# A mixture-of-experts block: first quad prepared ahead of the last choice, tables of experts in other places

## The chip, the cores and the metric

The kernel runs on one core of a Trainium2 chip. The metric is the device time of one execution in microseconds (us). The core's engines are TensorE (PE in the profile, its weight loads PEld), VectorE (DVE), ScalarE (ACT), GpSimd (POOL) and SyncE (SP); each runs its own program in order, and they wait for each other on semaphores. SPq and POOLq are the queues on which SyncE and GpSimd issue transfers.

## The reference, cut to what matters

```python
def attention(x):                      # x: (8, 64, 256), per image, after a normalisation over channels
    kq = w_kq @ x + b_kq; v = w_v @ x + b_v
    ctx = softmax(kq.T @ kq) @ v.T
    return w_o @ ctx + b_o
x = x + attention(ln_c(x))
t = tokens(x)                          # 2048 tokens of 64 channels
flat = ln_t(t)
probs = softmax(flat @ router_w.T)     # 8 experts
top 2 experts per token, their probabilities divided by their sum -> gates
y_e = w2[e] @ (silu(w1[e] @ flat) * (w3[e] @ flat))     # hidden 682, per chosen expert
t = t + sum over the two chosen e of gate_e * y_e
```

## The kernel before

**Attention stage.** The 8 images are handled in 4 pairs. Per pair `p`: statistics, transposes, the product `kq`, `similarity`, for each image `b` a `row_max(b)` on VectorE, `exponentials(b)` on ScalarE, `transpose_probs(b)` and `attend(b)` on TensorE, then on VectorE `residual(b)` (which gives the tokens and the router's logits), `t_statistics(p)`, `tops(b)`, `choose(p)`; TensorE's `rank(p)` counts each token's place within its expert, `positions(p)` makes row numbers, `normalise_t(p)` the normalised tokens. GpSimd computes the deviations (`t_deviation(p)`) and scatters the tokens with `scatter_row(p, at)`, 8 indirect transfers a pair, to a buffer `xs` in HBM that is sorted by expert.

**Expert stage.** The rows of `xs` are worked on in subtiles of 128 rows, each of one expert; there are up to 39, in 10 quads of four, and a round is the work on one quad. Round `i`: `pair_up(i)` on VectorE copies the loaded rows `x_in` twice side by side into `x_pairs`, `turn_x(i)` transposes them on TensorE, `columns(i)` copies them to `x_cols` on ScalarE. Then six steps `s` of `up(6i+s)` on TensorE, `silu` on ScalarE and `multiply` on VectorE, then `down(i)` on TensorE (L1061), ScalarE's `y_copy(i)` (L513), TensorE's `turn_y(i)`, VectorE's `results(i)` and GpSimd's four `scatter_result`. `up(g)` waits for the product `g-3`, so TensorE runs at most three steps ahead of VectorE.

**Tables.** Which expert a subtile has (`owners`), and where its rows begin (`rows`), is known as counts become known. There are three phases: after pair 1 eight subtiles (quads 0, 1), after pair 2 eight more (quads 2, 3), after pair 3 the rest. A phase's tables are VectorE chains of small operations: `subtiles_of_experts` (L659 to L670), `owners_of_slots` (L675, L678), `jumps_between_owners`, `rows_of_slots` (to L696 or L701), and `used_up` (L706, L707) ahead of a later phase. The first phase's are made at the start of pair 2, the second's at the end of pair 3 ahead of `pair_up(1)` and of `normalise_t(3)`, the third's in rounds 0 and 1.

**SyncE** waits for a phase's tables (`table_ready`) and reads row numbers and owners from the table into registers, four of each for a quad (`rows_of`, `owners_of`); it issues the four loads of rows (L293, 32.5 KB each) once the scatters of that phase have landed (`landed(p)`), and then the quad's four weight loads (L277, 565 KB each). There are buffers for the weights of three quads and the rows of four. All these transfers are on SyncE's queue.

**TensorE around the last choice.** After `attend(7)`: `keep_busy(4)` (products without a use, L959), `rank(3)`, `keep_busy(3)`, then `turn_x(0)`, `keep_busy(1)` and the rounds. `turn_x(i+1)` follows step 1 in round 0 and step 0 in later rounds, on ScalarE `columns(i+1)` likewise.

## Time and profile before

| | us |
|---|---|
| median of 3 runs | 174.97 |
| lowest, highest | 174.4, 175.56 |
| the profiled execution | 175.2 |
| its span | 173.1 |
| busy: PE, PEld | 144.0, 120.4 |
| busy: DVE, ACT, POOL | 97.8, 71.5, 85.7 |

The span is the time from the first to the last instruction that the profile holds; the device time has about 2 us more around it. An engine's busy share is an average over stages with different limits, so a change in a stage is read from that stage: from the instructions' order in time, and from the idle time ahead of them with the engine and line that ended it (`[0.83 <-DMA x_in<-xs]` is 0.83 us of idleness, ended by a transfer into x_in). PEclk is the granted clock of TensorE, 1.00 for 2.4 GHz and 0.50 for 1.2 GHz. Products in fp32 are pipelined, so that several overlap.

### The profile page before, as it was taken

To read this page: it belongs to the slowest core of one execution; us is meant where nothing else is said; L and a number is where in the kernel's file an instruction comes from. 1 tells how busy PE (TensorE), PEld (TensorE's weight loads), DVE (VectorE), ACT (ScalarE), POOL (GpSimd) and SP (SyncE) were. 2 spreads that over 40 slices of the span, in tenths; PEclk is the share of its full clock that TensorE was granted. 3 is DMA by queue.
4 is the path that set the end of the run, shared out by engine and by line. 5 is a ranking of instruction groups with operands and counts; after the bars stand their busy time and mean duration, and the time that the engine had idled before them with its cause. 6 is when DMAs were issued, how large, how long until landed. Compare 5 with 4: busy or idle time off the path is not lost.

```text
span 173.1 us, 4872 instructions
## 1 busy us (share of the span) xinstructions
PE 144.0 (83%) x1682; PEld 120.4 (70%) x1682; DVE 97.8 (57%) x364; ACT 71.5 (41%) x141; POOL 85.7 (50%) x114
## 2 busy tenths in 40 slices
PE   0669949578788699899699999999999999984782
PEld 0446737367277279797598989899999999874262
DVE  0645695785762888769554646455555736443050
ACT  2148666241144037253363636363545454542011
POOL 2685427887771477777071625344343526356000
PEclk9999997955555579999999999999999999999698
DMA  4999400100882492279896979596969981010434
GB/s 117 326 287 296 107 0 15 31 19 27 238 340 55 106 399 110 58 193 397 249 370 189 378 226 376 168 398 159 386 174 366 278 326 38 5 31 15 113 137 121
DMA packets 19892, 32.99 MB, mean 191 GB/s; under 512 B 7691, under 2 KB 13100, under 8 KB 19868
## 3 DMA queue, kind: packets, MB, share of 16 engines
q1 hardware_dynamic: 16732, 29.55, 52.6%
q0 software_dynamic: 2272, 2.35, 4.2%
q10 hardware_dynamic: 864, 0.79, 1.5%
q8 instruction: 13, 0.21, 0.5%
q14 instruction: 11, 0.09, 0.2%
HBM read 25.55 MB, written 7.13 MB: 189 GB/s over the span
## 4 chain that ended last, share of the span: by engine, by line
issue 30%; POOL 26%; PE 22%; DVE 9%; DMA 5%; ACT 5%; POOLq 1%; SPq 0%; DVEq 0%; ACTq 0%
POOL ys L366 20%; PE psum L927 7%; POOL xs L357 5%; PE psum L916 4%; PE psum L896 3%; ACT xn L422 2%; DMA y_in<-ys 2%; PE psum L1105 2%; PE psum L887 2%; DMA proj<-projections 1%; PE psum L882 1%; DMA ys<-y_out,y_row 1%; DVE parts L620 1%; ACT probsT L456 1%; DVE rows L591 1%
## 5 line engine op out<-in xcount | busy, mean ns | idle before, releaser
L366 POOL DMA_INDIRECT ys<-y_out,y_row x39 | 37.4, 958 | 45.3 <-DVE y_out L839 36.2
L1033 PE MATMUL psum<-x_cols,weights 64*128 64x128 f32 x390 | 49.5, 279 | 1.6 <-DMA weights<-experts 1.2
L1035 PE MATMUL psum<-x_cols,weights 64*128 64x128 f32 x390 | 49.7, 279 | 0.0
L1033 PEld LDWEIGHTS psum<-x_cols,weights 64*128 64x128 f32 x390 | 45.6, 188 | 5.7 <-issue 3.8
L827 DVE TENSOR_TENSOR hid<-psum,act_sb 128x512 f32<-128x512 f32 (+1 forms) x50 | 33.8, 677 | 23.4 <-ACT act_sb L500 23.1
L1035 PEld LDWEIGHTS psum<-x_cols,weights 64*128 64x128 f32 x390 | 45.7, 188 | 0.0
L500 ACT ACTIVATE act_sb<-psum 128x512 f32<-128x512 f32 (+1 forms) x50 | 29.3, 587 | 25.2 <-PE psum L1033 24.7
L357 POOL DMA_INDIRECT xs<-xrows,pos x32 | 31.6, 988 | 11.6 <-issue 8.6
L1061 PE MATMUL psum<-hid,weights 128*64 128x128 f32 x468 | 28.8, 276 | 0.2 <-DVE hid L827 0.2
L1061 PEld LDWEIGHTS psum<-hid,weights 128*64 128x64 f32 x468 | 25.9, 137 | 2.0 <-DVE hid L827 0.4
L927 PEld LDWEIGHTS psum<-u_sb,probsT 128*128 128x128 f32 x64 | 11.3, 266 | 5.2 <-ACT probsT L456 2.8
L927 PE MATMUL psum<-u_sb,probsT 128*128 128x73 f32 x64 | 12.3, 358 | 2.9 <-ACT probsT L456 1.6
L959 PE MATMUL psum<-ones,before 128*128 128x512 bf16 x24 | 10.3, 577 | 3.5 <-issue 3.5
L513 ACT COPY y_cols<-psum 128x256 f32<-128x256 f32 (+1 forms) x10 | 3.6, 362 | 21.2 <-PE psum L1061 21.2
L779 DVE COPY x_pairs<-x_in 128x512 f32<-128x512 f32 (+1 forms) x10 | 4.4, 438 | 11.0 <-DMA x_in<-xs 11.0
L448 ACT ACTIVATE probs<-psum,neg_max 128x256 f32<-128x256 f32 x16 | 6.7, 474 | 9.3 <-DVE neg_max L580 9.3
L492 ACT COPY x_cols<-psum 128x512 f32<-128x512 f32 (+1 forms) x10 | 5.7, 575 | 8.4 <-PE psum L1015 8.4
L456 ACT COPY probsT<-psum 128x512 f32<-128x512 f32 x8 | 4.7, 586 | 9.5 <-PE psum L916 9.5
L959 PEld LDWEIGHTS psum<-ones,before 128*128 128x128 bf16 x24 | 2.9, 133 | 7.9 <-issue 7.7
L916 PE MATMUL psum<-ident,probs 128*128 128x128 f32 x32 | 8.0, 401 | 0.3 <-ACT probs L448 0.3
L1015 PE MATMUL psum<-ident,x_pairs 128*128 128x128 f32 x39 | 6.9, 301 | 1.6 <-DVE x_pairs L779 1.6
L422 ACT ACTIVATE xn<-x_sb,shift_x,rstd 128x64 f32<-128x64 f32 x16 | 5.7, 428 | 5.9 <-DVE std L565 5.9
(147 smaller groups left out, 178.4 us busy)
## 6 DMA issues: line engine op xcount, KB each, us to landing
weights<-experts SPq DMA_DIRECT2D x39, 565.0 KB, 4.8
xs<-zeros SPq DMA_DIRECT2D x4, 1040.0 KB, 11.9
x_in<-xs SPq DMA_DIRECT2D x39, 32.5 KB
ys<-y_out,y_row POOLq DMA_INDIRECT x39
xs<-xrows,pos POOLq DMA_INDIRECT x32, 2.3
y_in<-ys ACTq DMA_DIRECT2D x2, 256.0 KB, 4.6
y_in<-ys SPq DMA_DIRECT2D x2, 256.0 KB, 4.4
x_sb<-x_tok SPq DMA_DIRECT2D x1, 384.0 KB, 3.8
```

Of the source, the lines that this page charges most:

```text
L357: nc.gpsimd.indirect_dma_start(xs, bass.IndirectOffsetOnAxis(ap=pos[:, p, at:at + 1], axis=0), xrows[:, TPP * p + at // K_TOP, at % K_TOP, ...
L366: nc.gpsimd.indirect_dma_start(ys, bass.IndirectOffsetOnAxis(ap=y_row[:, j:j + 1], axis=0), y_out[:, i % RING, h, :], None).then_inc(y_sca ...
L422: ins = nc.scalar.activation(xn[:, p, i, m, :], x_sb[:, t, :], ACT.Identity, bias=shift_x[:, t:t + 1], scale=rstd[:, t:t + 1])
L500: nc.scalar.activation(live(i, act_sb[:, g % 3, :]), live(i, H1_BANK[g % 2]), ACT.Silu).then_inc(silu_done, 1)
L827: nc.vector.tensor_tensor(live(i, hid[:, i % 2, s, :]), live(i, H3_BANK[g % 3]), live(i, act_sb[:, g % 3, :]), ALU.mult).then_inc(hid_done, 1)
L916: ins = nc.tensor.transpose(PT_BANK[:, N * j + P * i:N * j + P * (i + 1)], probs[:, b % 2, i, P * j:P * (j + 1)], ident[:])
L927: ins = nc.tensor.matmul(O_BANK[b % 2][:, (TX + 1) * i:(TX + 1) * (i + 1)], probsT[:, b % 2, j, P * i:P * (i + 1)], u_sb[:, 2 * b + j, E:] ...
L959: nc.tensor.matmul(bank[4], before[:], ones[:].unsqueeze(1).to_broadcast([P, BLK // P, P]), start=True, stop=True)
L1015: ins = nc.tensor.transpose(X_BANK[:, P * h:P * (h + 1)], x_pairs[:, i % 2, h, :, :], ident[:])
L1033: first_ = nc.tensor.matmul(H1_BANK[g % 2][:, src], weights[0:C, slot, P * s:P * (s + 1)], x_cols[0:C, i % 2, src], start=True, stop=True)
L1035: second_ = nc.tensor.matmul(H3_BANK[g % 3][:, src], weights[C:P, slot, P * s:P * (s + 1)], x_cols[C:P, i % 2, src], start=True, stop=True)
L1061: ins = nc.tensor.matmul(Y_BANK[C * (h % 2):C * (h % 2 + 1), P * (h // 2):P * (h // 2 + 1)], weights[:, slot, HP + C * s:HP + C * (s + 1)] ...
```

## The change

- The first phase's tables move from the start of pair 2 into pair 1, between the first two and the last two tiles of `normalise_t(1)`, and so ahead of `row_max(5)`.
- A new semaphore `owners_ready` rises when a phase's owners are known. SyncE loads the weights of quad 0 on it, one owner and one load at a time, and the weights of quad 2 on it, ahead of the row numbers and the row loads of quad 2.
- `pair_up(0)` moves ahead of `t_statistics(3)`; on TensorE `turn_x(0)` and `keep_busy(2)` come ahead of `rank(3)`; `keep_busy(3)` and `keep_busy(1)` go.
- The second phase's tables are made in pieces behind the products of steps 0 to 3 of round 0; `normalise_t(3)` moves behind step 5 of round 0. The third phase's `jumps` and `rows` move one step on in round 1.
- `pair_up(2)` moves from the end of round 0 behind step 2 of round 1; `turn_x(2)` and `columns(2)` move from step 0 to step 4 of round 1.
- GpSimd makes the deviation of pair 3 after all scatters of pair 2, where it was made after two of them.

```diff
@@ -54,6 +54,7 @@
 YROWS = PARK + NS * SUB
 WQUADS = 3
 WSLOTS = WQUADS * QUAD
+TURNED_AT = {0: 1, 1: 4}
 XRING = 4
 RING = 4
 ZW = E * CAP * RW // (QUARTERS * P * 8)
@@ -188,7 +189,7 @@
         dispatched = [sem(f"dispatched{p}") for p in range(PHASES)]
         variance_t_ready, rstd_t_ready = sem("variance_t_ready"), sem("rstd_t_ready")
         shifted, exponents, gates_ready = sem("shifted"), sem("exponents"), sem("gates_ready")
-        keep_ready, table_ready = sem("keep_ready"), sem("table_ready")
+        keep_ready, owners_ready, table_ready = sem("keep_ready"), sem("owners_ready"), sem("table_ready")
 
         w_loaded = [sem(f"w_loaded{i}") for i in range(WSLOTS)]
         x_in_loaded = [sem(f"x_in_loaded{i}") for i in range(XRING)]
@@ -295,21 +296,29 @@
             def landed(p):
                 sp.wait_ge(dispatched[p], 16 * TPP * K_TOP * (KNOWN[p] - (KNOWN[p - 1] if p else 0)))
 
+            sp.wait_ge(owners_ready, 1)
+            for h in members(0):
+                owner = sp.value_load(table[0:1, 0, h:h + 1], min_val=0, max_val=E - 1)
+                sp.dma_start(weights[:, h, :], experts[bass.ds(owner, 1)].rearrange("o p c -> p (o c)")).then_inc(w_loaded[h], 16)
             sp.wait_ge(table_ready, 1)
-            load_weights(0, owners_of(0))
             early_rows, second_owners = [rows_of(0), rows_of(1)], owners_of(1)
             landed(0)
             load_rows(0, early_rows[0])
             load_rows(1, early_rows[1])
             load_weights(1, second_owners)
             for p in range(1, PHASES):
+                sp.wait_ge(owners_ready, p + 1)
+                opening = quads_of(p)[0]
+                if opening < WQUADS:
+                    load_weights(opening, owners_of(opening))
                 sp.wait_ge(table_ready, p + 1)
                 for i in quads_of(p):
                     at = rows_of(i)
-                    if i == quads_of(p)[0]:
+                    if i == opening:
                         landed(p)
                     load_rows(i, at)
-                    load_weights(i, owners_of(i))
+                    if i >= WQUADS:
+                        load_weights(i, owners_of(i))
 
             all_scattered(sp)
             for q in range(0, QUARTERS, 2):
@@ -404,11 +413,11 @@
             t_deviation(0)
             for p in range(PAIRS):
                 for at in range(TPP * K_TOP):
-                    if p == 0 and at == TPP * K_TOP - 2 or p == 2 and at == K_TOP:
-                        t_deviation(p + 1)
+                    if p == 0 and at == TPP * K_TOP - 2:
+                        t_deviation(1)
                     scatter_row(p, at)
-                if p == 1:
-                    t_deviation(2)
+                if 1 <= p < PAIRS - 1:
+                    t_deviation(p + 1)
             for j in range(NS):
                 scatter_result(j)
 
@@ -521,7 +530,7 @@
                     y_copy(i - 1)
                 for s in range(STEPS):
                     silu(STEPS * i + s)
-                    if s == (1 if i == 0 else 0) and i + 1 < NQ:
+                    if s == TURNED_AT.get(i, 0) and i + 1 < NQ:
                         columns(i + 1)
             y_copy(NQ - 1)
             nc.scalar.preload_act_table(ACT.Exp)
@@ -623,9 +632,9 @@
                     ins = nc.vector.bn_aggr(moments_t[:, t, :], parts[:, 1, t, :])
                 ins.then_inc(moments_t_ready, 1)
 
-            def normalise_t(p):
+            def normalise_t(p, part=range(TPP)):
                 dve.wait_ge(rstd_t_ready, p + 1)
-                for t in range(TPP * p, TPP * (p + 1)):
+                for t in (TPP * p + i for i in part):
                     ins = nc.vector.tensor_scalar(xrows[:, t, :, 0:C], rows[:, t:t + 1, E:TX].to_broadcast([P, K_TOP, C]),
                                                   moments_t[:, t, 0:1], rstd_t[:, t:t + 1], ALU.subtract, ALU.mult)
                     ins.then_inc(tn_ready, 1)
@@ -675,8 +684,7 @@
                 chain(nc.vector.tensor_tensor(passed[:, own, :], slot_at[:, own].unsqueeze(2).to_broadcast([P, n, E - 1]),
                                               ends[:, 1:E].unsqueeze(1).to_broadcast([P, n, E - 1]), ALU.is_ge))
                 with nc.allow_low_precision(reason="numbers of experts: whole and below 2^3"):
-                    nc.vector.tensor_reduce(table[:, 0, own], passed[:, own, :], AX.X, ALU.add).then_inc(dve_step, 1)
-                steps[0] += 1
+                    nc.vector.tensor_reduce(table[:, 0, own], passed[:, own, :], AX.X, ALU.add).then_inc(owners_ready, 1)
 
             def jumps_between_owners(p):
                 if p == 0:
@@ -787,33 +795,31 @@
                     nc.vector.copy_predicated(y_row[:, own], keep[:, own], ids).then_inc(y_row_ready, 1)
 
             for p in range(PAIRS):
-                if p == KNOWN[0]:
-                    subtiles_of_experts(0)
-                    owners_of_slots(0)
-                    jumps_between_owners(0)
-                    rows_of_slots(0)
                 if p >= 1:
                     x_logits(p)
                 residual(2 * p)
                 tops(2 * p)
                 residual(2 * p + 1)
+                if p == PAIRS - 1:
+                    pair_up(0)
                 t_statistics(p)
                 if p + 1 < PAIRS:
                     row_max(2 * p + 2)
                 tops(2 * p + 1)
                 choose(p)
                 carry_on(p)
-                if p == PAIRS - 1:
-                    pair_up(0)
                 positions(p)
                 if p == PAIRS - 1:
-                    used_up(0)
-                    subtiles_of_experts(1)
-                    owners_of_slots(1)
-                    jumps_between_owners(1)
-                    rows_of_slots(1)
                     pair_up(1)
-                normalise_t(p)
+                if p == KNOWN[0] - 1:
+                    normalise_t(p, range(2))
+                    subtiles_of_experts(0)
+                    owners_of_slots(0)
+                    jumps_between_owners(0)
+                    rows_of_slots(0)
+                    normalise_t(p, range(2, TPP))
+                elif p < PAIRS - 1:
+                    normalise_t(p)
                 if p + 1 < PAIRS:
                     row_max(2 * p + 3)
 
@@ -840,14 +846,26 @@
                                       ).then_inc(y_out_ready, 1)
 
             def tables_between(i, s):
-                if (i, s) == (0, 5):
+                if (i, s) == (0, 0):
+                    used_up(0)
+                    subtiles_of_experts(1)
+                elif (i, s) == (0, 1):
+                    owners_of_slots(1)
+                elif (i, s) == (0, 2):
+                    jumps_between_owners(1)
+                elif (i, s) == (0, 3):
+                    rows_of_slots(1)
+                elif (i, s) == (0, 5):
+                    normalise_t(PAIRS - 1)
                     used_up(1)
                     subtiles_of_experts(2)
                 elif (i, s) == (1, 1):
                     owners_of_slots(2)
                 elif (i, s) == (1, 2):
+                    pair_up(2)
+                elif (i, s) == (1, 3):
                     jumps_between_owners(2)
-                elif (i, s) == (1, 3):
+                elif (i, s) == (1, 4):
                     rows_of_slots(2)
                 elif (i, s) == (1, 5):
                     occupancy(2)
@@ -860,7 +878,7 @@
                     if s == 0 and i >= 1:
                         results(i - 1)
                     tables_between(i, s)
-                if i + 2 < NQ:
+                if 1 <= i < NQ - 2:
                     pair_up(i + 2)
             results(NQ - 1)
 
@@ -1002,8 +1020,6 @@
                 if p + 1 < PAIRS:
                     similarity(p + 1)
             keep_busy(4)
-            rank(PAIRS - 1)
-            keep_busy(3)
 
             def turn_x(i):
                 pe.wait_ge(x_paired, i + 1)
@@ -1078,11 +1094,12 @@
             pe.wait_ge(probs_ready, B)
             pe.wait_ge(t_ready, B)
             turn_x(0)
-            keep_busy(1)
+            keep_busy(2)
+            rank(PAIRS - 1)
             for i in range(NQ):
                 for s in range(STEPS):
                     up(STEPS * i + s)
-                    if s == (1 if i == 0 else 0) and i + 1 < NQ:
+                    if s == TURNED_AT.get(i, 0) and i + 1 < NQ:
                         turn_x(i + 1)
                     if s == 0 and i >= 1:
                         turn_y(i - 1)
```

## Rows read from the trace of the kernel before

**Rows 1.** Timeline, ScalarE: the copy that closes a round (columns: start, duration, instruction, idle)

```profile
93.00 0.37 ACT L513 COPY y_cols<-psum 128x256 f32<-128x256 f32 x1 [2.05 <-PE psum L1061]
...
101.97 0.37 ACT L513 COPY y_cols<-psum 128x256 f32<-128x256 f32 x1 [2.05 <-PE psum L1061]
...
120.48 0.37 ACT L513 COPY y_cols<-psum 128x256 f32<-128x256 f32 x1 [2.05 <-PE psum L1061]
```

**Rows 2.** Windows: busy us (instructions) of each engine, PEclk, DMA share, GB/s

```profile
22.60:24.60 2.00, 0.00 (x0) 0.03 (x1) 1.86 (x14) 2.00 (x6) 1.27 (x2) 1.00 0.00 0
25.30:28.20 2.90, 2.76 (x12) 2.35 (x12) 2.04 (x8) 1.41 (x4) 1.58 (x2) 0.50 0.02 7
...
35.40:62.20 26.80, 21.77 (x109) 15.12 (x105) 18.40 (x105) 7.26 (x14) 16.56 (x18) 0.50 0.48 151
...
62.50:154.50 92.00, 88.83 (x1378) 82.01 (x1379) 55.01 (x124) 43.67 (x78) 45.93 (x48) 1.00 0.70 239
```

**Rows 3.** The page's part 5: pairing of the rows (busy, mean ns; idle before it)

```profile
L779 DVE COPY x_pairs<-x_in 128x512 f32<-128x512 f32 (+1 forms) x10 | 4.4, 438 | 11.0 <-DMA x_in<-xs 11.0
```

**Rows 4.** Timeline, SyncE's queue: loads of the rows and weights

```profile
68.64 2.58 SPq L293 DMA_DIRECT2D x_in<-xs  x4
73.62 2.16 SPq L277 DMA_DIRECT2D weights<-experts  x4
78.21 1.90 SPq L293 DMA_DIRECT2D x_in<-xs  x4
```

**Rows 5.** Timeline, VectorE: rounds 1 and 2

```profile
72.88 0.43 DVE L779 COPY x_pairs<-x_in 128x512 f32<-128x512 f32 x1 [0.83 <-DMA x_in<-xs]
...
77.78 0.16 DVE L685 TENSOR_TENSOR begin<-used,base 128x8 f32<-128x8 f32 x1
...
80.65 0.68 DVE L830 TENSOR_TENSOR hid<-psum,act_sb 42x512 f32<-42x512 f32 x1
...
84.53 0.43 DVE L779 COPY x_pairs<-x_in 128x512 f32<-128x512 f32 x1 [1.68 <-DMA x_in<-xs]
```

**Rows 6.** Timeline, TensorE: around rounds 0 to 2

```profile
55.93 1.91 PE L959 MATMUL psum<-ones,before 128*128 128x512 bf16 x4
...
62.48 0.46 PE L1033 MATMUL psum<-x_cols,weights 64*128 64x128 f32 x1 [0.25 <-ACT x_cols L492]
...
68.57 2.84 PE L1061 MATMUL psum<-hid,weights 128*64 128x128 f32 x48
...
83.24 0.34 PE L1033 MATMUL psum<-x_cols,weights 64*128 64x128 f32 x1 [1.21 <-DMA weights<-experts]
```

**Rows 7.** Timeline, VectorE: the end of pair 1 and the first tables

```profile
36.17 1.11 DVE L629 TENSOR_SCALAR xrows<-rows,moments_t,rstd_t 128x128 f32<-128x128 f32 x4
37.19 0.68 DVE L580 TENSOR_REDUCE neg_max<-psum 128x2 f32<-128x512 f32 x1
37.79 0.28 DVE L659 SCALAR_TENSOR_TENSOR over<-taken_by,steps_sub 128x128 f32<-128x128 f32 x1
...
40.01 0.17 DVE L696 TENSOR_TENSOR table<-row_at,slot_at 128x8 int32<-128x8 f32 x1
```

**Rows 8.** Timeline, ScalarE: exponentials of image 5, first silu

```profile
38.16 0.85 ACT L448 ACTIVATE probs<-psum,neg_max 128x256 f32<-128x256 f32 x2
...
63.75 0.60 ACT L500 ACTIVATE act_sb<-psum 128x512 f32<-128x512 f32 x1 [1.33 <-PE psum L1033]
```

**Rows 9.** Chain that ended last: transposes of image 5

```profile
40.31 0.87 PE psum L916 x4
```

**Rows 10.** Timeline, VectorE: last choice, tables of phase 1, first products

```profile
58.90 0.19 DVE L614 TENSOR_TENSOR taken<-chosen 128x32 bf16<-128x32 f32 x1
...
60.31 0.16 DVE L706 TENSOR_SCALAR given<-ends 128x8 f32<-128x8 f32 x1
...
62.33 0.21 DVE L678 TENSOR_REDUCE table<-passed 128x8 int32<-128x56 f32 x1
...
65.32 1.27 DVE L827 TENSOR_TENSOR hid<-psum,act_sb 128x512 f32<-128x512 f32 x2
```

## The prediction

> **What bounds the kernel now.** Read the copies that close a round first: one round is the work on one quad of subtiles, and ScalarE copies its output at the end [rows 1]. From 93.00 to 101.97 a round takes 8.97 us, and TensorE has no gap in it: the windows view shows 88.83 us busy of 92 from 62.5 to 154.5, at full clock [rows 2]. So ten rounds, most of them bound by TensorE. The next two rounds, 101.97 to 120.48, take 18.51 where 2 x 8.97 = 17.94 would do. They lose 0.57 us. The page's costliest groups say to what: VectorE stood 11.0 us in all for x_in, the rows of the coming quads [rows 3].
>
> So read SyncE's queue [rows 4]. Per quad it reads four row numbers, issues four row loads (x_in), reads four owners, issues four weight loads. From the end of the weights at 73.62 + 2.16 = 75.78 to 78.21 lie the four register loads: 2.43 us, 0.61 each. A whole turn (row loads 1.90, weights 2.16, twice 2.43 and the wake-ups) is 9 to 9.5 us, as long as a round or longer: a second, hidden bound. A quad's rows come late as well, for they are issued behind the previous quad's weights: those of quad 3 are issued from 78.21 and VectorE gets them at 84.53, 6.3 us later [rows 5]. The rows of quad 2, issued from 68.64 with no weights ahead of them, were there at 72.88, 4.2 us later [rows 4, 5].
>
> Third, the places that lose time around the first rounds. TensorE starts round 0 at 62.48, ends it at 68.57 + 2.84 = 71.4, and starts round 2 at 83.24, held 1.21 us by weights [rows 6]. GpSimd's scatters of pair 2 stop in the middle, behind a deviation whose moments are late.
>
> **The change, part by part.** (1) *First tables ahead of row_max(5).* The tables take 37.79 to 40.18, 2.39 us [rows 7]. They now lie between two halves of normalise_t(1) (1.11 us for four, so 0.57 a half), and row_max(5) is queued behind all: 36.17 + 0.57 + 2.39 + 0.5 gives 39.6, plus 0.66 gives 40.25, where it ended at 37.87. Who waits: the exponentials of image 5 ran at 38.16 for 0.85 [rows 8] and now run at 40.28 to 41.12; the transposes of them started at 40.31, set by TensorE [rows 9], and now start at 41.16. The cover was 1.3 us, the delay is 2.4: all that follows in the attention stage comes **0.85 us later**, since this is the chain of waits. SyncE gets the first owners 1 us earlier and issues the first weights and rows earlier; nobody waited for either (rounds 0 and 1 show no wait for them), so this gains 0.
>
> (2) *pair_up(0) ahead of t_statistics(3)*: 0.43 and a copy of ids, 0.46 us together, on VectorE [rows 5], earlier, so the last choice comes 0.85 + 0.46 = 1.31 later: taken at 58.90 + 0.19 + 1.31 = 60.40 [rows 10].
>
> (3) *TensorE.* keep_busy(4) ended at 57.84 [rows 6], now 58.7. turn_x(0) follows directly (about 0.9), ScalarE's copy ends at about 60.2, keep_busy(2) fills until 60.4, rank(3) starts at 60.55 and takes 0.35. Round 0 starts at **60.9 instead of 62.48**, 1.6 us sooner. That is the visible gain.
>
> (4) *Tables of phase 1 between the products of round 0.* VectorE: positions 0.5 from 60.95, pair_up(1) 0.5, then silu(0) (63.75 + 0.60 was 1.87 after the round's start [rows 8]) ends at 62.8. multiply(0) 0.62, as two took 1.27 [rows 10]; used_up and subtiles; multiply(1) 0.62; owners. The two table parts were 60.31 to 62.54, 2.23 us [rows 10]. So owners_ready rises at 62.8 + 0.62 + 2.23 + 0.62 = **66.25**. The products are then late by the tables' time; round 0 ends on VectorE's last product at about 70.9 against 71.4. Of 1.6 us only 0.5 is left here. Then normalise_t(3) (1.1) and used_up(1) with subtiles(2) (2.0) delay the first product of round 1 to 73.3.
>
> (5) *SyncE's order.* From 66.25: four owners 2.65 (with the wake-up), four weights 2.15, four row numbers 2.43, so the rows of quad 2 are issued from **73.5; before, from 68.64** [rows 4]. The weights of quad 2 leave at 68.9 instead of 73.62, and the 1.21 us wait at 83.24 goes. But the rows are now behind 2.26 MB of weights. With the 6.3 us of quad 3's rows they are there at **79.8**. The bounds: 4.2 us, as in the empty queue (77.7), and 7.0 (80.5).
> The Trainium skill, "DMA: Bandwidth & Descriptors", section "Queues, rings and completion order", says that descriptors of one ring are consumed in ring order, which speaks against this reordering; by it the small rows wait for all the weights, as the trace's 6.3 us shows, and the sum is the one made here.
>
> (6) *turn_x(2) after step 4 of round 1, pair_up(2) after step 2.* VectorE reaches pair_up(2) at 73.3 + three products, results and owners(2) = 76.2 and stands until 79.8. Queued behind it are the products of steps 3, 4 and 5 and the tables of phase 2. Before, jumps, three products and rows took 77.78 to 80.65 + 0.68 = 81.33 [rows 5], 3.55 us; now 79.8 + 0.41 + 3.55 = 83.8, and the last sixth of down(1) (2.84 / 6) gives 84.3. TensorE has done up of steps 0 to 4 by 75.9 and stands until 80.25: **a gap of 4.3 us that was not there.**
>
> (7) *GpSimd.* The stop in pair 2 is closed, but pair 3's scatters now wait for normalise_t(3) at 71.3 and end at 81.4, 4 us later than before; results of quad 0 follow until 86.5, ahead of quad 1's. SyncE needs the scatters at 87. Worth 0 while these covers hold; without them each scatter is 1.26 us.
>
> **What the gap costs.** A gap of 2.0 us (22.6 to 24.6) was followed by a clock of 0.50, that is 1.2 GHz, although TensorE was 95% busy after it; work was back at 24.6 and 28.2 still shows 0.50, so the low clock held for 3.6 us of work or a little more [rows 2]. So a gap of 4.3 us most likely brings 1.2 GHz. Work left in round 1 at 80.25: transposes 0.5, tail 0.6, down 2.84 = 3.95 us at full clock. Each us at half clock does half a us. If the clock returns 3 to 4 us after work resumes (I take 3.6), the round ends at 80.25 + 3.95 + 1.8 = **86.0**. Hot it would be 84.3, by VectorE.
> The Trainium skill, "TensorE: Matmul & The Clock Gate", section "HAM oscillation — how this bites in real kernels", has waits for DMA bring the half clock as well; the trace's much shorter gap agrees. By that rule the sum stays the one with the half clock.
>
> **The sum.** Round 2 starts at 86.0; quad 3's rows are issued at 77.85 and are long there. Round 2 takes 8.97 and closes at 95.0; before at 93.00: +2.0. SyncE's issues from quad 3 on stay where they were (77.85 against 78.21), so with TensorE later its two late row loads no longer show: -0.57. The end moves by **+1.4 us**. The profiled execution took 175.2 us with a span of 173.1, so 176.6; against the median 174.97 it is 0.2 slow. Forecast 174.97 + 1.4 = **176.4 us**.
>
> **Rivals.** *A, the clock stays up*: 84.3, then quad 3's pairs at 85.7 hold the turn 0.5 us, round 2 closes at 93.75, +0.75 - 0.57 = +0.2: 175.2. For it: full clock since 62.5. Against: the 2.0 us gap. *B, the rows of quad 2 are not held by the weights* (77.7 or sooner): no long gap, round 2 starts at 82 or earlier. But then TensorE runs into SyncE's turn in rounds 3 to 5, and SyncE is only 0.35 us ahead of before: 174.6. Against: 6.3 us at 84.53. *C, the other side, slower by over 1%: the half clock lasts.* Place: down(1), after the gap. Price: 0.5 us per us. It decides from 4.3 us of half clock on, where the sum passes +1.75; until 86.9 it gives +2.95, and if round 0 also starts at half clock (60.9 lies in the stretch that ran at 0.50, [rows 2]) VectorE's first product, and all behind it, is 0.75 later: +3.7, 178.7. Typical 177.6. For it: from 35.4 to 62.2 the clock stayed at 0.50 with TensorE busy 21.77 of 26.8 us. *D, faster by over 1%*: the 1.6 us of the start and the losses of rounds 1 and 2 (83.24 - 62.48 - 2 x 8.97 = 2.8) are all kept: up to 170.6. For it: the weights wait goes. Against: SyncE's turn would have to shrink too, and it is four loads and four issues twice over as before.
>
> **How the numbers follow.** Forecast 0.36, A 0.10, B 0.06, C 0.38, D 0.10. One per cent, 1.75 us, is about what a measurement tells here. Forecast, A and B are within it: 0.52; C slower: 0.38; D faster: 0.10. The range runs from B, 174.6, less nothing, to C with nearly all its terms, 178.4; it leaves out D and the rest of C, under 0.2. The likeliest case's own range is 175.9 to 176.7.
>
> **What would show it.** Right: the transposes of image 5 at 41.2; up of round 0 at 60.9; weights of quad 2 issued at 69 and its rows at 73.5; x_pairs waiting over 3 us for x_in before 80 in round 1; a TensorE gap of 4 us there and a clock below 1.00 behind it; round 2 starting between 85 and 87; no x_in wait on TensorE in rounds 4 and 5. Wrong: rows of quad 2 there by 78; owners_ready before 65; SyncE's turn under 9 us; round 6 starting before 120.

## The result and the profile after

| | us |
|---|---|
| median before, 20 runs | 176.65 (173.26 to 180.43) |
| median after, 20 runs | 177.84 (174.97 to 180.70) |
| ratio after / before | 1.0099, 95% interval 1.0051 to 1.0148 |
| profiled execution after, its span | 178.76, 177.0 |

The change makes the kernel about 1% slower; 0.8% was forecast (1.4 us of 174.97). Over 20 runs both kernels scatter by 3 to 4%, so the ratio, not the two medians, is the result. The ratio and its interval, here and below, compare only the executions of each kernel that lie within 1.5% of its fastest; the medians of all 20 stand at 1.0067.

The profiled execution of after has 3.9 us more span than that of before; it is read for where time goes, not for how much in the median. Only 2.36 us of the 3.9 are there at the end of round 5. The other 1.5 lie behind the last round, where the 32 transposes of the result took 5.34 us instead of 3.84, at a granted clock of 0.50 until 171.7. That isn't the change: a second profile of after has them at 3.84 again.

The profiled executions differ by up to 2.3 us (31.0 to 33.3) at the start of residual(3), ahead of all that was changed. So marks are also counted from one of their own execution, **residual(7)**: the start of VectorE's work on image 7, the last, at 56.24 before and at 56.81 after.

```profile
56.24 0.17 DVE L586 RECIPROCAL inv_sum<-psum 128x2 f32<-128x2 f32 x1 [2.11 <-PE psum L927]
```

```profile
56.81 0.17 DVE L595 RECIPROCAL inv_sum<-psum 128x2 f32<-128x2 f32 x1 [2.11 <-PE psum L945]
```

ScalarE's copies that close a round in the kernel after, which answer to [rows 1]:

```profile
70.25 0.37 ACT L522 COPY y_cols<-psum 128x256 f32<-128x256 f32 x1 [2.42 <-PE psum L1077]
...
86.96 0.37 ACT L522 COPY y_cols<-psum 128x256 f32<-128x256 f32 x1 [4.19 <-PE psum L1077]
...
95.93 0.37 ACT L522 COPY y_cols<-psum 128x256 f32<-128x256 f32 x1 [2.05 <-PE psum L1077]
...
104.90 0.37 ACT L522 COPY y_cols<-psum 128x256 f32<-128x256 f32 x1 [2.05 <-PE psum L1077]
...
122.84 0.37 ACT L522 COPY y_cols<-psum 128x256 f32<-128x256 f32 x1 [2.05 <-PE psum L1077]
```

Before closed its first two rounds here:

```profile
71.46 0.37 ACT L513 COPY y_cols<-psum 128x256 f32<-128x256 f32 x1 [2.05 <-PE psum L1061]
...
82.08 0.37 ACT L513 COPY y_cols<-psum 128x256 f32<-128x256 f32 x1 [2.67 <-PE psum L1061]
```

Round 0 closes at 70.25. Round 1 closes at 86.96, 16.7 us later, where before needed 10.6. From then on every round takes 8.97 us: round 2 closes at 95.93, 2.9 us behind before's 93.00, and round 5 at 122.84, 2.36 us behind 120.48. The 0.57 us that before lost in rounds 4 and 5 is what came back.

SyncE's queue after, against [rows 4] (the first row is the weights of quads 1 and 2, the second the rows of quads 2 and 3, merged by the view):

```profile
54.02 16.37 SPq L278 DMA_DIRECT2D weights<-experts  x8
72.81 6.29 SPq L294 DMA_DIRECT2D x_in<-xs  x8
81.50 2.16 SPq L278 DMA_DIRECT2D weights<-experts  x4
```

The rows of quad 2 are issued at 72.81, 4.2 us later than before. VectorE after, around the last choice, in round 0 and in round 1, against [rows 10] and [rows 5]:

```profile
57.52 0.42 DVE L787 COPY x_pairs<-x_in 128x512 f32<-128x512 f32 x1
...
59.76 0.19 DVE L623 TENSOR_TENSOR taken<-chosen 128x32 bf16<-128x32 f32 x1
...
62.25 0.69 DVE L833 TENSOR_TENSOR hid<-psum,act_sb 128x512 f32<-128x512 f32 x1 [0.76 <-ACT act_sb L509]
...
65.46 0.21 DVE L687 TENSOR_REDUCE table<-passed 128x8 int32<-128x56 f32 x1
...
74.62 0.68 DVE L833 TENSOR_TENSOR hid<-psum,act_sb 128x512 f32<-128x512 f32 x1
79.29 0.44 DVE L787 COPY x_pairs<-x_in 128x512 f32<-128x512 f32 x1 [4.00 <-DMA x_in<-xs]
...
82.80 0.68 DVE L836 TENSOR_TENSOR hid<-psum,act_sb 42x512 f32<-42x512 f32 x1
```

pair_up(0) is at 57.52, ahead of the choice (taken at 59.76). The owners are known at 65.46 + 0.21 = 65.67. In round 1 VectorE ends a product at 75.3 and stands 4.00 us for x_in, in the middle of the round; the round's last product comes at 82.80. TensorE after, against [rows 6]:

```profile
60.46 0.34 PE L1049 MATMUL psum<-x_cols,weights 64*128 64x128 f32 x1
...
79.79 1.11 PE L1031 MATMUL psum<-ident,x_pairs 128*128 128x128 f32 x4 [4.29 <-DVE x_pairs L787]
```

Round 0 begins at 60.46, and in round 1 TensorE stands for the pairs until 79.79, 4.29 us by the row. Windows after (us, busy of PE, PEld, DVE, ACT, POOL with instructions, granted clock, DMA share, GB/s), against [rows 2]:

```profile
76.00:79.70 3.70, 0.00 (x0) 0.00 (x0) 0.41 (x2) 0.12 (x1) 2.79 (x4) 0.97 0.68 196
80.00:86.00 6.00, 6.00 (x50) 5.41 (x51) 5.18 (x18) 1.18 (x2) 4.08 (x5) 0.50 0.63 200
...
86.50:154.00 67.50, 67.50 (x1067) 62.69 (x1064) 36.09 (x68) 33.96 (x62) 28.38 (x30) 1.00 0.71 242
```

TensorE is idle to 79.7; then come 6 us of work without a break at 0.50, 1.2 GHz, and 1.00, 2.4 GHz, from 86.5 on. Cut finer, the windows show the clock fall at 79.5, while TensorE still stood, and come back at 86.3. The last sixth of down(1) could have come behind VectorE's last product at 83.5; it ended at 86.9.

Ends of rounds behind residual(7), in us, for the kernels that the text turns on. "Filled" and "GpSimd's order" are experiments below.

| | profiles | round 1 | round 2 | round 5 |
|---|---|---|---|---|
| before | 1 | 25.8 | 36.8 | 64.2 |
| after | 2 | 30.2, 29.7 | 39.1, 38.7 | 66.0, 65.6 |
| after, gap filled | 2 | 27.4, 27.9 | 36.6, 37.1 | 63.5, 64.0 |
| after, GpSimd's order back | 2 | 27.8, 29.2 | 36.8, 38.2 | 63.7, 65.1 |
| before, GpSimd's order alone | 1 | 25.2 | 34.3 | 61.4 |

### The profile page after: what moved, and what is told of

The parts are those of the page before. It is cut to its first block, busy times and chain, and to the rows that moved or that the text cites. A ratio compares the mean times of both kernels' runs of the same rounds, so it can differ in the third digit from the quotient of the medians.

```text
span 177.0 us, 4868 instructions
## 1 busy us (share of the span) xinstructions
PE 146.8 (83%) x1680; PEld 124.1 (70%) x1680; DVE 97.2 (55%) x364; ACT 71.4 (40%) x141; POOL 86.2 (49%) x114
## 4 chain that ended last, share of the span: by engine, by line
issue 30%; POOL 24%; PE 21%; DVE 12%; ACT 5%; DMA 4%; POOLq 1%; SPq 0%; DVEq 0%; ACTq 0%
POOL ys L375 20%; PE psum L945 6%; POOL xs L366 4%; PE psum L934 4%; PE psum L1122 3%; ACT xn L431 2%; DMA y_in<-ys 2%; PE psum L914 2%; DVE hid L833 2%; PE psum L905 2%; PE psum L900 1%; DMA ys<-y_out,y_row 1%; DMA proj<-projections 1%; ACT probsT L465 1%; DVE neg_max L589 1%
## 5 line engine op out<-in xcount | busy, mean ns | idle before, releaser
L833 DVE TENSOR_TENSOR hid<-psum,act_sb 128x512 f32<-128x512 f32 (+1 forms) x50 | 33.9, 677 | 33.3 <-ACT act_sb L509 32.9
L1077 PE MATMUL psum<-hid,weights 128*64 128x128 f32 x468 | 30.8, 288 | 0.0
L1077 PEld LDWEIGHTS psum<-hid,weights 128*64 128x64 f32 x468 | 28.1, 145 | 1.9 <-issue 0.3
L977 PE MATMUL psum<-ones,before 128*128 128x512 bf16 x22 | 8.1, 514 | 3.5 <-issue 3.5
L1031 PEld LDWEIGHTS psum<-ident,x_pairs 128*128 128x128 f32 x39 | 4.7, 156 | 6.1 <-DVE x_pairs L787 4.5
```

The lines of the kernel that those rows point to most:

```text
L833: nc.vector.tensor_tensor(live(i, hid[:, i % 2, s, :]), live(i, H3_BANK[g % 3]), live(i, act_sb[:, g % 3, :]), ALU.mult).then_inc(hid_done, 1)
L977: nc.tensor.matmul(bank[4], before[:], ones[:].unsqueeze(1).to_broadcast([P, BLK // P, P]), start=True, stop=True)
L1031: ins = nc.tensor.transpose(X_BANK[:, P * h:P * (h + 1)], x_pairs[:, i % 2, h, :, :], ident[:])
L1077: ins = nc.tensor.matmul(Y_BANK[C * (h % 2):C * (h % 2 + 1), P * (h // 2):P * (h // 2 + 1)], weights[:, slot, HP + C * s:HP + C * (s + 1)] ...
```

## The experiments

All ratios are to the kernel before, measured beside it. A difference between two of them is read with both intervals in mind.

**The gap filled.** In the kernel after, TensorE runs 16 products without a use in the gap:

```diff
+                    if (i, s) == (1, 4):
+                        pe.wait_ge(x_cols_ready, 2)
+                        for _ in range(16):
+                            nc.tensor.matmul(X_BANK, before[:], ones[:].unsqueeze(1).to_broadcast([P, BLK // P, P]),
+                                             start=True, stop=True)
                     if s == TURNED_AT.get(i, 0) and i + 1 < NQ:
                         turn_x(i + 1)
```

> The changed kernel with 16 products without a use put on TensorE between step 4 of round 1 and turn_x(2), that is into the 4 us gap. Theory (the gap costs by its half clock): the granted clock stays 1.00 through rounds 1 and 2, round 1 closes at about 84.5 instead of 86.96, set by VectorE's last product, round 2 at about 93.9; time against the kernel before 1.001 to 1.003. Rival (the late rows alone cost the time, the clock does not matter): round 1 closes at 86.5 or later as in the changed kernel, ratio 1.01.

Measured: 1.0030 (0.9967 to 1.0094). A window and the close of round 1 in it:

```profile
80.00:86.00 6.00, 5.44 (x77) 4.61 (x78) 5.49 (x20) 1.84 (x4) 4.35 (x5) 1.00 0.58 171
...
84.63 0.37 ACT L522 COPY y_cols<-psum 128x256 f32<-128x256 f32 x1 [2.22 <-PE psum L1077]
```

The clock stays at 1.00 over the whole round. VectorE still stands 4.06 us for x_in and makes the pairs at 79.91, later than after's 79.29, yet the round closes 2.3 us sooner: 4.7 us behind the pairs instead of 7.7. So between these two profiles 3 us of round 1 are the clock's. The late rows by themselves leave round 1 closing 27.4 us behind residual(7), where before closed it after 25.8. But that is made up again: round 2 closes at 36.6 (before 36.8) and round 5 at 63.5 (before 64.2). The gap without its half clock costs nothing by round 5, and what is left of the loss is made ahead of residual(7), by the first tables (1.06 us, below).

A second time, beside the kernel after itself:

> The changed kernel with the TensorE gap of round 1 filled, a second time, beside the changed kernel. Theory (the half clock behind the gap is most of the loss): 0.5 to 1.2 per cent below the changed kernel, clock 1.00 through rounds 1 and 2. Rival: the same as the changed kernel.

> The changed kernel itself, beside the next two on one chip. Theory: a TensorE gap of about 4 us in round 1 and 3.4 to 6.8 us of half clock behind it, the length by chance from execution to execution; ratio 1.003 to 1.012.

Measured: filled 1.0035 (0.9980 to 1.0091), after 1.0050 (1.0000 to 1.0099). The order is the expected one both times, but the second difference, 0.15%, is less than expected and far inside the intervals; over both sessions it is 0.4% (1.0033 against 1.0075). The second profiles say the same as the first: filled, the clock stays at 1.00 and round 1 closes 5.0 us behind its pairs; in after TensorE stands 3.75 us, the clock is 0.50 from 80.2 to 87.0, and the round closes 7.4 us behind its pairs. That the half clock happens and what it costs in one execution is shown by the profiles; what share of the median it is stays uncertain.

**First tables back behind row_max(5)**, all else as after:

```diff
             for p in range(PAIRS):
+                if p == KNOWN[0]:
+                    subtiles_of_experts(0)
+                    owners_of_slots(0)
+                    jumps_between_owners(0)
+                    rows_of_slots(0)
                 if p >= 1:
                     x_logits(p)
...
-                if p == KNOWN[0] - 1:
-                    normalise_t(p, range(2))
-                    subtiles_of_experts(0)
-                    owners_of_slots(0)
-                    jumps_between_owners(0)
-                    rows_of_slots(0)
-                    normalise_t(p, range(2, TPP))
-                elif p < PAIRS - 1:
+                if p < PAIRS - 1:
                     normalise_t(p)
```

> The changed kernel with the first phase's tables back behind row_max(5). Theory (the tables delay row_max(5) and by it the attention stage by 0.85 us): the transposes of image 5 start with no wait for the exponentials, all later marks 0.8 to 1 us earlier, ratio 1.003 to 1.005. Rival (the sooner first tables pay by earlier weights and rows of quads 0 and 1): ratio above 1.01, a wait on weights or rows in round 0 or 1.

Measured: 0.9988 (0.9930 to 1.0045). Starts of residual(4) and residual(5) on VectorE, of before, of after and then of this kernel:

```profile
40.42 0.16 DVE L586 RECIPROCAL inv_sum<-psum 128x2 f32<-128x2 f32 x1
...
43.93 0.17 DVE L586 RECIPROCAL inv_sum<-psum 128x2 f32<-128x2 f32 x1 [2.02 <-PE psum L927]
```

```profile
39.93 0.16 DVE L595 RECIPROCAL inv_sum<-psum 128x2 f32<-128x2 f32 x1
...
44.50 0.17 DVE L595 RECIPROCAL inv_sum<-psum 128x2 f32<-128x2 f32 x1 [3.09 <-PE psum L945]
```

```profile
41.27 0.16 DVE L595 RECIPROCAL inv_sum<-psum 128x2 f32<-128x2 f32 x1
...
44.71 0.17 DVE L595 RECIPROCAL inv_sum<-psum 128x2 f32<-128x2 f32 x1 [1.97 <-PE psum L943]
```

From 39.93 to 44.50 are 4.57 us; from 41.27 to 44.71, 3.44. Before had 3.51. So the tables ahead of row_max(5) cost 1.1 us in the chain, and nothing was gained by having them sooner: no wait for the weights or rows of quads 0 and 1 shows up here. The ratio fell by 1.1%, more than the 0.6% that 1.1 us is, and below the 1.003 to 1.005 expected; the intervals leave room for that. Its profile also had a shorter half clock in round 1, 80.5 to 84.0, against 79.5 to 86.3 in after's, which this edit doesn't explain; so the 1.1% need not be all the tables'.

**Second phase's tables back in one piece** ahead of pair_up(1), all else as after:

> The changed kernel with the second phase's tables back in one piece at the end of pair 3, ahead of pair_up(1); all else as changed. Theory (late tables make the rows of quad 2 late): owners_ready about 2 us earlier (near 63.5), rows of quad 2 issued near 71 instead of 72.8 and paired near 77.2 instead of 79.3, the TensorE gap in round 1 about 2 us instead of 4, end 2 us or more earlier than the changed kernel, ratio 0.995 to 1.000. Rival (pieces cost nothing, since the weights of quad 2 set the end of round 1): ratio 1.01 as the changed kernel.

Measured: 1.0241 (1.0148 to 1.0335), a miss. The owners were known sooner (6.4 us behind residual(7), against 8.9 in after), and the rows of quad 2 came without a wait (pairs at 80.64, 21.6 us behind residual(7), against 22.5 in after). But pair_up(1) stood behind the tables until 66.78, and TensorE, which now starts round 0 early, stood 2.6 us for it and worked at half clock behind it: round 0 closed at 75.67, 16.7 us behind residual(7) instead of 13.4. normalise_t(3), which stays behind round 0, went with it. GpSimd's first scatter of pair 3, and SyncE's weight loads of quad 3 and row loads of quad 4, which wait for these scatters (3.2 us, by the view of SyncE's waits from 84 to 95; none in after):

```profile
74.89 1.27 POOL L366 DMA_INDIRECT xs<-xrows,pos  x1 [11.25 <-DVE xrows L638]
...
80.89 2.04 SPq L278 DMA_DIRECT2D weights<-experts  x4
90.08 2.97 SPq L294 DMA_DIRECT2D x_in<-xs  x4
```

The scatters begin 15.9 us behind residual(7) instead of 13.2, the rows of quad 4 are issued at 90.08, their weights behind them, and TensorE stands 2.49 us for the weights of quad 4: round 3 closes at 103.51, round 4 at 115.06, 11.55 us later. So the pieces in round 0 do buy something, once TensorE starts early: they let pair_up(1) and the products through. The kernel tests both together and does not price the pieces alone.

**SyncE's order for quad 2 back**, rows first, tables left as after:

```diff
-                if opening < WQUADS:
-                    load_weights(opening, owners_of(opening))
                 sp.wait_ge(table_ready, p + 1)
...
-                    if i >= WQUADS:
-                        load_weights(i, owners_of(i))
+                    load_weights(i, owners_of(i))
```

> The changed kernel with SyncE's order for quad 2 as before: its rows first, on table_ready, then its weights; the tables stay in pieces and late. Theory (what is late is SyncE's whole turn, since owners and rows of phase 1 are known later; the order only chooses who waits): rows of quad 2 issued near 70.5 and paired near 75.5 without a stall of VectorE, but the weights of quad 2 issued near 75 and landed near 83.5 to 84.5, so TensorE waits over 2.5 us for them at the start of round 2; ratio 1.005 to 1.015. Rival (the order of the two loads is what costs): no wait above 1 us in rounds 1 and 2, ratio below 1.0.

Measured: 1.0176 (1.0098 to 1.0255), a little above the range expected. SyncE's issues, and TensorE's start of round 2:

```profile
71.19 1.89 SPq L294 DMA_DIRECT2D x_in<-xs  x4
75.48 2.08 SPq L278 DMA_DIRECT2D weights<-experts  x4
```

```profile
86.16 0.55 PE L1046 MATMUL psum<-x_cols,weights 64*128 64x128 f32 x1 [5.74 <-DMA weights<-experts]
```

The rows are issued 14.0 us behind residual(7) instead of 16.0 and are paired at 75.64 without a wait; round 1 closes at 80.47. Then TensorE stands 5.74 us for the weights, and the clock is 0.50 from 83.1 to 89.9. So the swap in SyncE's order is not the fault: with tables this late the new order is no worse, and by the ratios (1.0176 against 1.0099 and 1.0050) the better of two. What is late is SyncE's whole turn.

**GpSimd's order alone**, in the kernel before:

```diff
-                    if p == 0 and at == TPP * K_TOP - 2 or p == 2 and at == K_TOP:
-                        t_deviation(p + 1)
+                    if p == 0 and at == TPP * K_TOP - 2:
+                        t_deviation(1)
...
-                if p == 1:
-                    t_deviation(2)
+                if 1 <= p < PAIRS - 1:
+                    t_deviation(p + 1)
```

> The kernel before with only GpSimd's order changed: the deviation of pair 3 after all scatters of pair 2. Theory (SyncE's turn is a second bound, and it started late because the scatters of pair 2 landed at 68.6): rows of quad 2 issued near 66.4 instead of 68.6, all of SyncE's issues 2.2 us earlier, no weights wait at the start of round 2, rounds from 3 on closing 2 to 2.5 us earlier, ratio 0.985 to 0.99. Rival (TensorE alone is the bound): only the start of round 2 changes, by at most 1.2 us, ratio 0.994 to 1.000.

Measured: **0.9846 (0.9764 to 0.9927), faster than both kernels**; median 172.75. SyncE's queue and the rounds' copies:

```profile
65.87 1.89 SPq L293 DMA_DIRECT2D x_in<-xs  x4
70.17 1.92 SPq L277 DMA_DIRECT2D weights<-experts  x4
74.53 1.93 SPq L293 DMA_DIRECT2D x_in<-xs  x4
78.86 2.34 SPq L277 DMA_DIRECT2D weights<-experts  x4
84.03 1.90 SPq L293 DMA_DIRECT2D x_in<-xs  x4
```

```profile
80.94 0.37 ACT L513 COPY y_cols<-psum 128x256 f32<-128x256 f32 x1 [2.67 <-PE psum L1061]
...
90.05 0.37 ACT L513 COPY y_cols<-psum 128x256 f32<-128x256 f32 x1 [2.05 <-PE psum L1061]
...
99.02 0.37 ACT L513 COPY y_cols<-psum 128x256 f32<-128x256 f32 x1 [2.05 <-PE psum L1061]
```

Before, the first three of these issues were at 68.64, 73.62, 78.21, and SyncE's row loads waited for scatters, 2.3 us of it ahead of 68.64:

```profile
SPq L293 <- DMA xs<-xrows,pos: 2.8, 2, 2.3
```

(us in total, times, the longest.) With GpSimd's order changed no such wait is left ahead of the rows of quad 2, the weights of quad 2 are there in time, and round 2 closes at 90.05 instead of 93.00, 34.3 us behind residual(7) instead of 36.8. A change of a few lines on GpSimd, which was busy for half of the span, is worth 2.7 us, because SyncE's turn hangs on it. The two experiments below that hold this order as well gave 0.986 and 0.983.

**GpSimd's order back in the kernel after**, twice:

> The changed kernel with GpSimd's order as before (deviation of pair 3 after two scatters of pair 2). Theory (in the changed kernel the scatters of pair 2 have landed long before SyncE gets to the rows of quad 2 at 72.8, so the new order brings nothing there): pair 2's scatters end near 68.5, the rows are still issued near 72.8, rounds close as in the changed kernel, ratio 1.005 to 1.015. Rival (GpSimd's order is worth its 1.5 per cent in the changed kernel too): ratio 1.02 or more.

> The changed kernel with GpSimd's order as before, a second time, beside the changed kernel. Theory (the order brings nothing there; the first ratio of 0.998 came from a shorter half clock in those executions): the same ratio as the changed kernel within 0.006. Rival (the new order costs the changed kernel something): again 0.8 to 1.2 per cent below it.

Measured: 0.9978 (0.9926 to 1.0031), then 1.0038 (0.9983 to 1.0093) beside after's 1.0050. In the profiles the rows of quad 2 are issued at 73.42 and 74.61, 16.0 and 16.6 us behind residual(7), as in after (16.0). So in the kernel after the order brings nothing: pair 2's scatters are not what SyncE waits for ahead of these rows. The rival, a ratio of 1.02 or more, is refuted. The first ratio lay below the range expected and 1.2% under after's; in that profile the clock was 0.50 from 79.9 to 83.3 only, against 79.5 to 86.3 in after's. Side by side the difference was gone, and the second profile had 79.1 to 85.9.

**The start alone** (pair_up(0), turn_x(0), keep_busy(2) and rank(3) moved as in the change), in the kernel before, and with GpSimd's order:

> The kernel before with the start alone (pair_up(0) ahead of t_statistics(3), turn_x(0) and keep_busy(2) ahead of rank(3)). Theory: as with GpSimd's order beside it, round 0 starts 1.5 to 2 us sooner and closes no sooner, SyncE's issues stay where they were or 0.3 us later, ratio 1.000 to 1.008. Rival (the start is gained): ratio 0.992 or lower.

> The kernel before with two parts of the change: GpSimd's order, and the start (pair_up(0) ahead of t_statistics(3), turn_x(0) and keep_busy(2) ahead of rank(3)); all tables as before. Theory (the second bound is SyncE and VectorE's tables, so an earlier start of round 0 brings nothing): round 0 starts 1.5 to 2 us sooner, TensorE then stands over 2 us for the pairs of quad 1, which wait behind the tables, tables and SyncE are 0.46 us later, and the end is 0.3 to 1.5 us later than with GpSimd's order alone, ratio 0.987 to 0.995. Rival (the start is gained): ratio 0.978 or lower.

Measured: 0.9996 (0.9959 to 1.0033) and 0.9861 (0.9790 to 0.9933), so the start is worth nothing on either while the tables stay in one piece. TensorE in the second:

```profile
64.61 0.66 PE L1013 MATMUL psum<-ident,x_pairs 128*128 128x128 f32 x4 [2.53 <-DVE x_pairs L779]
```

It starts round 0 early and then stands 2.53 us for the pairs of quad 1, which wait behind the tables on VectorE. Round 0 closes 15.35 us behind residual(7), where before closed it after 15.22.

**The attention stage filled**: GpSimd's order, and `keep_busy(12)` instead of `keep_busy(3)` ahead of the ranks of pairs 1 and 2:

> The kernel before with GpSimd's order, and with 12 products without a use instead of 3 ahead of the ranks of pairs 1 and 2, in the two places of the attention stage where TensorE stands 2.3 and 1.2 us for VectorE's choice. Theory (a gap of 2 us and more brings the half clock, as in round 1 of the changed kernel, and the half clock from 35 to 62 costs more than the gap itself): the clock stays 1.00 from 28 to 60, the attention stage ends 2 us or more earlier, ratio 0.965 to 0.98. Rival (the attention stage is set by the chain over VectorE and ScalarE, or its products do not hold the clock anyway): the clock falls near 38 to 45 all the same, then the added products at half clock delay the ranks by about 2 us, ratio 0.99 to 1.005.

Measured: 0.9831 (0.9749 to 0.9914), no different from GpSimd's order alone. Windows and TensorE in it:

```profile
33.00:41.00 8.00, 6.15 (x47) 3.73 (x43) 7.30 (x40) 3.28 (x7) 6.06 (x7) 1.00 0.07 21
42.00:44.50 2.50, 2.50 (x13) 1.12 (x13) 2.19 (x18) 0.00 (x0) 1.89 (x3) 0.50 0.09 27
45.00:51.50 6.50, 4.59 (x35) 2.97 (x33) 3.48 (x19) 1.85 (x4) 4.99 (x6) 1.00 0.93 342
52.00:64.00 12.00, 8.99 (x44) 5.71 (x46) 7.85 (x51) 3.09 (x5) 8.02 (x9) 0.50 0.50 139
```

```profile
43.48 3.52 PE L959 MATMUL psum<-ones,before 128*128 128x512 bf16 x12
...
52.68 1.11 PE L916 MATMUL psum<-ident,probs 128*128 128x128 f32 x4 [2.28 <-ACT probs L448]
```

Neither theory held as put. The clock was up for most of 33 to 51.5, and residual(4) to residual(5) took 1.5 us (41.27 to 42.79) instead of 3.5. But most of it was given back at 52.68, where TensorE stood 2.28 us for the exponentials of image 7: residual(6) to residual(7) took 4.56 us instead of 3.58. These wait for row_max(7) behind normalise_t(2), whose deviation GpSimd computes only after pair 1's scatters (the power ends at 50.0 here, and at 49.4 before). With that gap the half clock was back, from 51.9 on. By this reading GpSimd's queue is the next bound of the attention stage; no run tests it.

## Why the prediction was right, step by step

- *Tables ahead of row_max(5), 0.85 us.* Right in place and cause; 1.06 us in after's profile (4.57 - 3.51), 1.1 us by undoing it.
- *The start, 1.6 us sooner.* Forecast 3.8 us behind residual(7), measured 3.65 (60.46 - 56.81); before 6.24. Round 0 closed 13.4 us behind residual(7), against 15.2 before, somewhat sooner than forecast (70.9 - 57.1 = 13.8). Start and pieces of tables do this together: the start with the tables in one piece closed round 0 after 15.4 us, without a gain in time. What was gained in round 0 was lost in the wait of round 1, as forecast.
- *Owners at 66.25, the rows issued at 73.5, there at 79.8.* Measured 65.67, 72.81 and 79.29. The 6.3 us behind the weights, taken from one row of before, was 6.5, against the 4.2 us of an empty queue; over the second profile of after and those of the filled gap it ran from 5.7 to 7.3.
The rule of the Trainium skill that the descriptors of a ring are consumed in order ("DMA: Bandwidth & Descriptors", section "Queues, rings and completion order") agrees with this.
- *A stall of 3.6 us on VectorE and of 4.3 us on TensorE.* Measured 4.00 and 4.29.
- *The half clock returns after 3.6 us of work.* The mechanism is right, its size differs from execution to execution. In both profiles of after the clock was 0.50 for 6.8 us, most of it work; in the profiled one round 1 closed at 86.96 and not at 86.0, and the end was +2.36 us at round 5, near rival C's. With GpSimd's order back it was 3.4 us once and 6.8 once. From the pairs to the close of round 1 took 4.7 and 5.0 us at full clock, 6.2 with the short half clock, 7.0 to 7.7 with the long one: it costs about 1.3 or 2 to 3 us, where the sum has 1.7 (86.0 - 84.3).
- *The size of the sum, +1.4 us.* Here luck has a part. Counted as 1.06 us of tables ahead of residual(7) and the rest from the table above, the profiles of after are 2.4 and 2.9 us slower than before at round 5, and the one with the short half clock 0.5 us. None is the forecast's execution; it lies between them, and so does the median (1.0% is 1.75 us). The forecast gave 1.2 us of its 1.4 to the half clock (176.4 against rival A's 175.2); the filled gap gives it 0.4%, 0.7 us, with intervals that allow 0 as well as 1.2.
- *The rivals.* A fell with the clock of 0.50 in both profiles of after, B with the 4.00 us wait, D with the ratio. C is the forecast's mechanism with the longer half clock. Its other term, a round 0 that starts at half clock, wasn't there in the profiled execution (1.00 from 59.1 on), but it was in the second, where the clock came back at 63.1, 1.0 us after round 0 had begun, and round 0 closed 0.6 us later.
- *Recovery of 0.57 us in rounds 4 and 5.* Measured 0.57 (2.93 at round 2, 2.36 at round 5).
- *What the prediction did not see.* It gave GpSimd's order nothing, which holds in the kernel after, and did not say what it would be worth by itself. The issue at 68.64 was 2.2 us later than tables and register loads explain (the tables were done at 63.97, and 2.43 us of loads make 66.4), and that wait was for the scatters that the stop in pair 2 delays. The change closed this stop and at the same time made the tables 4 us later, so that the gain went under. That is where the time of the change's good part went.

## What to carry to other kernels

Before spreading a chain of small operations between products, ask which queue starts on its result, and follow that queue to the end of its turn: here the tables were late for SyncE, not for VectorE. A wait that is put into the middle of a round stops TensorE, VectorE and ScalarE in it, and if it leaves TensorE idle for some microseconds it can be paid twice, in the gap and in the half clock behind it; here the gap of 4 us by itself was made up by round 5, and the half clock was not. Try the parts of a change one by one: GpSimd's order alone gave -1.5%, the start alone nothing, the sooner first tables cost 1.1 us, and the whole was +1%.

## What the runs showed of the hardware

A half clock has no fixed price. In seven profiles a gap of TensorE in rounds 0 to 2 was followed by a clock of 0.50:

| | gap, us | clock 0.50 from, to | length | work is back at |
|---|---|---|---|---|
| after | 4.29 | 79.5, 86.3 | 6.8 | 79.79 |
| after, second | 3.75 | 80.2, 87.0 | 6.8 | 81.43 |
| GpSimd's order back, second | 3.70 | 79.1, 85.9 | 6.8 | 80.66 |
| rows first | 5.74 | 83.1, 89.9 | 6.8 | 86.16 |
| GpSimd's order back, first | 3.42 | 79.9, 83.3 | 3.4 | 79.59 |
| first tables back | 3.89 | 80.5, 84.0 | 3.5 | 79.66 |
| second tables in one piece | 2.56 | 67.5, 71.0 | 3.5 | 67.26 |

Where the clock fell while TensorE still stood, it stayed low for 6.8 us; where it fell after work was back, for about 3.4. And gaps of 2.61 and 2.53 us in round 0, in the kernels with the start alone and with the start and GpSimd's order, left it at 1.00, while 2.56 us, above, did not: near that length the gap alone doesn't say whether the clock falls.

Both kernels, before and after, spread by 3 to 4% over 20 runs of the same program. One part is seen at the end: from the last copy of the last round to the end of the span are 18.0 to 18.1 us in eleven of the fourteen profiles and 19.6 to 19.8 in three (after, filled gap, attention stage filled), where the last 32 transposes took 5.3 to 5.5 us with the clock at 0.50 for most of them, instead of 3.84. Another is the attention stage, which shows its low clock over stretches of different length. How much of the spread these explain was not measured.
